# Where weighing stands among the score products, and one slot's delay of the low parts, in a five-layer attention kernel

## The chip, the cores and the metric

The program runs on 1 core of one Trainium2 chip. The time is the device time of one execution in microseconds. PE is TensorE, DVE is VectorE, ACT is ScalarE, POOL is GpSimd, SP is SyncE, which issues the DMA transfers.

## What is computed

x has 32 sequences of 128 tokens with 128 features. Five attention layers with 16 heads of 8 features follow each other, with a perceptron after the second and the last, and a routed mixture of three experts between the second and the third:

```python
def _attn(q, k, v, mask):
    s = jnp.einsum('bqhd,bkhd->bhqk', q, k) * scale
    s = jnp.where(mask, s, jnp.finfo(s.dtype).min)
    a = jax.nn.softmax(s, axis=-1)
    return jnp.einsum('bhqk,bkhd->bqhd', a, v)
```

l0: self attention with rotary positions and a query-key mask (128 keys). l0c: cross attention to 77 context tokens, with a key mask. l2: cross attention, 77 keys, no mask. l3s: self attention, 128 keys, no mask. l3c: cross attention, 77 keys, no mask. The layers with 128 keys are called wide here, those with 77 narrow. Each layer is x + attention(norm(x)) times its output weights, in f32.

## The kernel before, in words

One sequence of one layer is a job; four jobs are a quad. There are 8 quads a layer and 40 in all, 160 jobs. Every engine runs the same loop over slots t. In slot t the exact scores of job t are made; qi is t // 4 and cl is t % 4. All engines have their instructions in an order written out by hand, and semaphores join them. Phase 0 is l0 and l0c, phase 1 the other three; the routed mixture lies between.

A job goes through these steps:

- POOL `spread_k(t+7)` (L1952) puts the keys of one job into a block form, `kblk_r`, which has two buffers.
- PE `rows(t+5, 1)` and `rows(t+6, 0)` (L658, in l0c also L653, in l0 with `mask_rows`, L634) make the row scores of heads 8 to 15 of one job and heads 0 to 7 of the next. Both use the same two banks of PSUM, `row_scores`.
- DVE `row_max` (L1242) takes the negated maximum of each row. The next use of the banks waits for it.
- Once a quad, ACT rounds the maxima (L1738), POOL splits off their low part, PE turns them (`turn_max`, L666) and DVE spreads them (`spread_max`, L1249).
- PE `exact(t)` (L695, 16 products of 32 rows) and `shift(t, h)` (L710) make the scores with the row maximum subtracted, in l0 with `mask_scores` (L676). `exact(t)` waits until ACT has taken both halves of job t-1.
- ACT `exponentiate(t, h)` (L1758) takes half 0 and half 1, 1024 columns each.
- PE `weigh(t-1)` (L725, 32 products) multiplies with the values; DVE `turn_blocks` (L1258), `invert` (L1263) and `turn_back` (L1270), and POOL `normalise(t-2)` (L1995) follow.
- `quad_work` on PE has what comes once a quad: projections of k for quad qi+2 at cl 0 (L605), of v (L613) and of the output (L620) at cl 2, of q for quad qi+3 at cl 3 (L594), the transposes of norms at cl 1, some at cl 3 (L572). In the wide layers the function `quad_ahead` does a part of it, half projections among them, between the subtractions and the row scores.

The exact scores are made from high and low parts of q and k. ACT `round_q` (L1673, cl 1) and `round_k(qi+2)` (L1683, cl 3, between the two exponentials of that slot) make the high parts; POOL `split_q` (L1935) and `split_k` (L1943) subtract them to get the low ones. There is one buffer each for `k_high`, `q_low` and `k_low`. SP `stack_pair(m)` (L2157, L2160) then copies high and low parts of two jobs into a ring of three pairs with 8 transfers; it waits for both splits of the quad. `round_k` and `split_q` of the next quad wait for the landing of both pairs of this quad:

```python
def round_k(q):
    w.wait_ge(k_split, q)
    if q:
        w.wait_ge(*pair_landed(2 * q - 2))
        w.wait_ge(*pair_landed(2 * q - 1))
```

In POOL's slot the order is: rotated halves of l0 (`add_rotated`, L1959, L1962, at cl 0 and 1), `spread_k(t+7)`, `split_max` (cl 2), `normalise(t-2)`, the two splits, `shift_normed` (L1983), `normalise_x` (L1969, L1972; for the norm that PE turns at cl 1 it stands in cl 0), sums into x.

Of the kernel before, what the change touches and what calls it, by code (L numbers as in the profile page):

```python
# [17 lines left out]
B, S, D = 32, 128, 128  # L18
# [72 lines left out]
def layer_of(q):  # L91
    return LAYERS[q // NB]
# [92 lines left out]
def build(nc, a, out_x):  # L185
    with ExitStack() as ctx:
# [343 lines left out]
        def tensor_program(e):  # L530
# [26 lines left out]
            def keep_busy(times, bank):  # L557

                for _ in range(times):
                    e.matmul(bank, ident, W["ones"], start=True, stop=True)  # L560
# [191 lines left out]
            def attention(phase, first=-16, last=None):  # L752
# [32 lines left out]
                        else:  # L785
                            w.wait_ge(q_done, qi + 3 - NB + 1)

                def is_wide(t):

                    return t in jobs and layer_of(t // QUAD).nk == S  # L790

                def quad_ahead(qi, cl):

                    for back in range(1, QUAD + 1):
                        quads_read(QUAD * qi + cl - back)
                    if cl == 0 and qi + 2 in quads:
                        project_k(qi + 2, slice(0, 2))
                    if cl == 2 and qi - 2 in quads:
                        project_out(qi - 2)
                    if cl == 3 and qi + 3 in quads:  # L800
                        project_q(qi + 3, slice(0, QUAD if layer_of(qi).rope else 2))

                def quad_work(t, qi, cl):
                    early = max(min(2 * t + 1, 8 * hi), 8 * lo)
                    if cl == 2 and qi + 1 in quads:
                        w.wait_ge(exp_done, early)
                        project_v(qi + 1)
                    if t in norm_at and not turned_in_quads(norm_at[t]):
                        w.wait_ge(exp_done, early)
                        turn_normed(norm_at[t])  # L810
                    if t == -2 * QUAD:
                        project_k(0)
                    if cl in (0, 3) or t in norm_at or cl == 1 and qi + 3 in quads or cl == 2 and qi - 2 in quads:
                        for back in range(1, QUAD + 1):
                            quads_read(t - back)
                    rest = slice(2 if is_wide(t) else 0, QUAD)
                    if cl == 0 and qi + 2 in quads and t != -2 * QUAD:
                        project_k(qi + 2, rest)
                    if cl == 1 and qi + 3 in quads and layer_of(qi + 3).name == "l3c":
                        turn_x(qi + 3)  # L820
                    if t in norm_at and turned_in_quads(norm_at[t]):
                        turn_normed(norm_at[t])
                    if cl == 2 and qi - 2 in quads and not is_wide(t):
                        if qi >= hi:
                            w.wait_ge(exp_done, early)
                        project_out(qi - 2)
                    if cl == 3 and qi + 3 in quads and not (is_wide(t) and layer_of(qi).rope):
                        project_q(qi + 3, rest)

                for t in range(4 * lo + first, end):  # L830
                    qi, cl = divmod(t, QUAD)
                    masked = t in jobs and layer_of(qi).mask == "qk"
                    if t + 5 in jobs:
                        mask_rows(t + 5, 1, True)
                    if t in (4 * lo, 4 * lo + 1):
                        w.wait_ge(max_done, 8 * lo + 8)
                    if masked:
                        scores_read(t - 1)
                        mask_scores(t, 0)
                    if t + 5 in jobs:  # L840
                        rows(t + 5, 1)
                    scores_read(t - 1)
                    if t in jobs:
                        exact(t)
                        shift(t, 0)
                        shift(t, 1)
                    if is_wide(t):
                        quad_ahead(qi, cl)
                    if phase == 1 and t in (4 * lo - 2, 4 * lo - 1):
                        keep_busy(4, av_bank[:, 0:128])  # L850
                    if t + 6 in jobs:
                        rows(t + 6, 0)
                    if masked:
                        mask_rows(t + 6, 0, False)
                        mask_scores(t, 1)
                        if cl == 3 and qi + 1 in quads:
                            w.wait_ge(nblk_done, qi + 2)
                    if masked or is_wide(t) and cl == 2:
                        quad_work(t, qi, cl)
                        if t - 1 in jobs:  # L860
                            weigh(t - 1)
                    else:
                        if t == 4 * hi:
                            first_layer(phase, 0, hi, range(2))
                        if t - 1 in jobs:
                            weigh(t - 1)
                        if t + 6 in jobs:
                            mask_rows(t + 6, 0, False)
                        if t in (-6, -4, -3):
                            keep_busy(3, scores[:, 0, 0:128])  # L870
                        if cl == 3 and qi + 1 in quads:
                            turn_max(qi + 1)
                        quad_work(t, qi, cl)
                    if masked and cl == 2 and qi + 1 in quads:
                        turn_max(qi + 1)
                    if phase == 0 and last is None:
                        first_prototypes(t - 4 * hi)
                    if t == -11:
                        modulate(range(2, 9))
                    if t == -8:  # L880
                        gates_and_context()
                    if t == -7:
                        w.wait_ge(act_setup, ACT_AT["l0mod1"])
                        keep_busy(5, scores[:, 0, 0:128])
                    c = first_layer_at(t, hi)
                    if c is not None:
                        first_layer(phase, c, hi, range(0 if c else 2, 4))
                    if second_layer_at(t, hi) is not None:
                        second_layer(phase, second_layer_at(t, hi), hi)
                    if phase == 0 and folding_at(t, hi) is not None:  # L890
                        fold_weights(folding_at(t, hi))
# [1020 lines left out]
        def pool_program(e):  # L1912
# [102 lines left out]
            def attention(phase, first=-16, last=None):  # L2015
# [4 lines left out]
                for t in range(4 * lo + first, end):  # L2020
# [8 lines left out]
                        split_max(qi + 1)  # L2029
                    if t - 2 in jobs:  # L2030
                        normalise(t - 2)
                    if cl == 3 and qi + 2 in quads:
                        split_q(qi + 2)
                        split_k(qi + 2)
                    if t - 1 in norm_at and not affine_by_act(norm_at[t - 1]):
                        shift_normed(norm_at[t - 1])
                    for it in XHAT_AT.get((phase == 1, t), ()):
# [278 lines left out]
```

## Time and profile before

| | us |
|---|---|
| median of 3 runs | 1069.88 |
| lowest and highest | 1067.48, 4715.3 |
| the profiled execution | 1063.98 |
| its span | 1061.8 |
| mean granted TensorE clock | 0.952 |

The profiled execution's own time is 2.2 us more than the span from its first to its last instruction. The clock has two levels, 2.4 GHz (1.00) and 1.2 GHz (0.50). In a timeline row the number after the start is the duration; in brackets stand the idle time of the engine before the row and what ended it.

### The profile page before, as it was taken

What the parts mean: (1) busy time and instruction counts of PE and PEld (TensorE: products, weight loads), DVE (VectorE), ACT (ScalarE), POOL (GpSimd) and SP (SyncE); (2) the same over time, 40 slices, a digit from 0 to 9 for tenths busy, and PEclk for the clock granted to TensorE, in tenths of its full rate; (3) what the DMA queues carried; (4) which work ended last, traced back from release to release, by engine and by line L of the source; (5) the groups of instructions that cost most, each with busy time, mean ns of one, the idle gap of its engine ahead of it and who ended that gap; (6) DMA issues with size and microseconds to landing.
All of it is one profiled execution on the core that took longest, in us unless ns stands there. A gap on an engine that the chain in (4) does not pass through costs nothing.

```text
span 1061.8 us, 32084 instructions
## 1 busy us (share of the span) xinstructions
PE 971.6 (91%) x13009; PEld 670.9 (63%) x13009; DVE 749.7 (71%) x1852; ACT 623.6 (59%) x938; POOL 616.5 (58%) x739
## 2 busy tenths in 40 slices
PE   7898898998889999999999988888999998888998
PEld 5455565666566776676776655655666666566676
DVE  7767888777875444677787768877898766776421
ACT  2144455577767555545554567775677677775752
POOL 6657888576874332111113779776778655685520
PEclk9569999999997999999999989998999999997999
DMA  6613333434332102000000133333334333333011
GB/s 215 219 65 112 120 108 107 133 107 134 125 120 74 41 30 98 9 10 7 7 7 19 59 116 107 123 107 103 131 112 145 116 125 119 110 98 121 7 40 40
DMA packets 101459, 96.89 MB, mean 91 GB/s; under 512 B 11632, under 2 KB 93808, under 8 KB 100928
## 3 DMA queue, kind: packets, MB, share of 16 engines
q1 hardware_dynamic: 101312, 94.84, 26.9%
q8 instruction: 103, 1.69, 0.7%
q14 instruction: 44, 0.36, 0.1%
HBM read 18.77 MB, written 2.15 MB: 20 GB/s over the span
## 4 chain that ended last, share of the span: by engine, by line
PE 68%; DVE 14%; issue 8%; POOL 7%; ACT 1%; SPq 1%; DMA 0%; POOLq 0%; DVEq 0%; ACTq 0%
PE weighed L725 13%; DVE negmax L1242 8%; PE row_scores L658 8%; PE scores L921 6%; PE weighed L748 5%; PE scores L613 4%; PE row_scores L921 3%; PE quads L620 3%; POOL kblk_r L1952 3%; PE quads L594 2%; PE row_scores L738 2%; PE scores L738 2%; PE quads L605 2%; PE row_scores L634 2%; PE weighed L938 2%
## 5 line engine op out<-in xcount | busy, mean ns | idle before, releaser
L1242 DVE TENSOR_REDUCE negmax<-row_scores 128x8 f32<-128x616 f32 (+1 forms) x312 | 298.5, 957 | 101.4 <-PE row_scores L658 74.4
L1758 ACT ACTIVATE p<-scores 128x1024 f32<-128x1024 f32 (+1 forms) x253 | 253.1, 1019 | 123.4 <-PE scores L710 87.7
L1952 POOL TENSOR_TENSOR kblk_r<-work,pack_const 128x308 fp32r<-128x308 f32 (+1 forms) x160 | 133.6, 836 | 113.0 <-PE row_scores L658 92.1
L658 PE MATMUL row_scores<-kblk_r,qr 32*128 32x308 f32 (+1 forms) x624 | 145.5, 457 | 52.4 <-DVE negmax L1242 42.4
L725 PE MATMUL weighed<-p,v 77*32 77x128 f32 (+1 forms) x5120 | 184.4, 288 | 1.8 <-DVE nat L1258 1.3
L725 PEld LDWEIGHTS weighed<-p,v 77*32 77x32 f32 (+1 forms) x5120 | 137.9, 114 | 36.1 <-issue 27.2
L658 PEld LDWEIGHTS row_scores<-kblk_r,qr 32*128 32x128 f32 x624 | 63.9, 191 | 130.2 <-issue 84.6
L695 PE MATMUL scores<-q_ring,k_ring 32*77 32x128 f32 (+1 forms) x2512 | 123.0, 256 | 4.4 <-ACT shared L1695 1.7
L695 PEld LDWEIGHTS scores<-q_ring,k_ring 32*77 32x77 f32 (+1 forms) x2512 | 100.0, 167 | 7.9 <-ACT shared L1695 1.9
L1258 DVE STREAM_TRANSPOSE nat<-weighed 128x256 f32<-128x256 f32 x160 | 70.9, 443 | 41.8 <-PE weighed L725 37.1
L710 PE MATMUL scores<-nblk,select 32*77 32x512 bf16 (+1 forms) x628 | 93.1, 396 | 0.0
L1995 POOL TENSOR_TENSOR attn<-nat,rden 128x128 f32<-128x128 f32 x160 | 64.7, 404 | 43.4 <-DVE rden L1263 41.2
L1758 ACT ACTIVATE p<-scores,neg_kb 77x1024 f32<-77x1024 f32 x61 | 65.8, 1105 | 15.8 <-PE scores L710 12.9
L1969 POOL TENSOR_TENSOR xh<-x,mv 128x512 f32<-128x512 f32 x48 | 50.0, 1041 | 25.6 <-ACT rst L1657 25.6
L748 PEld LDWEIGHTS weighed<-layers_w,work 128*128 128x128 f32 x512 | 59.0, 192 | 3.6 <-issue 2.4
L1972 POOL TENSOR_TENSOR xh<-xh,rst 128x512 f32<-128x512 f32 (+1 forms) x56 | 58.2, 1040 | 4.4
L748 PE MATMUL weighed<-layers_w,work 128*128 128x128 f32 x512 | 59.9, 275 | 0.8 <-DVE x L1299 0.8
L2068 POOL TENSOR_TENSOR xh<-x,r_mv 128x512 f32<-128x512 f32 x8 | 8.3, 1042 | 80.5 <-ACT r_rst L1665 79.6
L1935 POOL TENSOR_TENSOR work<-work,qr 128x512 f32<-128x512 f32 x40 | 50.8, 1270 | 4.9 <-DMA q_ring<-qr 4.9
L594 PE MATMUL quads<-work,layers_w 128*128 128x512 f32 (+1 forms) x96 | 48.3, 586 | 0.0
L1746 ACT COPY v<-scores 77x512 f32<-77x512 f32 (+1 forms) x40 | 23.3, 583 | 37.1 <-PE scores L613 37.0
L1131 DVE BATCH_NORM_STATS2 bn<-x 128x6 f32<-128x128 f32 x192 | 43.9, 268 | 0.6 <-POOL x L2007 0.6
(334 smaller groups left out, 1958.1 us busy)
## 6 DMA issues: line engine op xcount, KB each, us to landing
q_ring<-work SPq DMA_DIRECT2D x160, 128.0 KB, 2.1
q_ring<-qr SPq DMA_DIRECT2D x160, 128.0 KB, 2.1
k_ring<-k_high SPq DMA_DIRECT2D x64, 128.0 KB, 2.1
k_ring<-work SPq DMA_DIRECT2D x64, 128.0 KB, 2.1
k_ring<-k_high SPq DMA_DIRECT2D x96, 77.0 KB, 2.0
k_ring<-work SPq DMA_DIRECT2D x96, 77.0 KB, 2.0
shared<-gates_hbm SPq DMA_DIRECT2D x24, 256.0 KB, 3.1
shared<-in_ctx_tok SPq DMA_DIRECT2D x15, 154.0 KB
```

The lines of the kernel that those rows point to most:

```text
L594: mm = e.matmul(quad_bank[:, at], W[layer.wq], xn[q % 3][:, at], start=True, stop=True)
L658: mm = e.matmul(row_banks(n, h)[:, i, 0:cols], qr[q % 3][at, s * S:(s + 1) * S], kblk_r[n % 2][at, 0:cols], start=layer.mask is None or ma ...
L695: mm = e.matmul(score_banks(n, g // 2)[0:nk, g % 2, j * S:(j + 1) * S], keys_of(m, nk)[at, j, half * nk:(half + 1) * nk].bitcast(F32R), q_ ...
L710: mm = e.matmul(score_banks(n, h)[0:nk, i, :], select[at, s, 0:nk], nblk[q % 2][at, :], start=False, stop=not masked_after, skip_group_che ...
L725: mm = e.matmul(av_bank[TILE * j:TILE * j + TILE, i2 * S:(i2 + 1) * S], v[0:nk, at:at + TILE], p[n % 2][0:nk, g * NJ + j, :], start=i1 == ...
L748: mm = e.matmul(mlp_out_bank[:, s * D:(s + 1) * D], mlp_h[c % 2][k][:, s * S:(s + 1) * S], W[weight][:, k * D:(k + 1) * D], start=(k == 0) ...
L921: mm = e.matmul(bank, weight, src, start=(part == 0), stop=(part == 1))
L1242: e.tensor_reduce(negmax[q % 2][:, 2 * h:2 * h + 2, s * NJ:(s + 1) * NJ], row_banks(n, h)[:, :, 0:NJ * nk].rearrange("p g (j k) -> p g j k ...
L1258: e.transpose(nat[n % 2][:, :, :].rearrange("p c (i s) -> p (c i) s", i=NG), av_bank[:, weighed_cols].rearrange("p (i b s) -> p b i s", i= ...
L1758: e.activation(p[n % 2][0:nk, 8 * h:8 * h + 8, :], score_banks(n, h)[0:nk].rearrange("p g (j q) -> p (g j) q", j=NJ), ACT.Exp, bias=hide, ...
L1952: e.tensor_tensor(kblk_r[n % 2][:, 0:NJ * nk].rearrange("p (j k) -> p j k", j=NJ), k_of[q % 2][:, s * nk:(s + 1) * nk].unsqueeze(1).to_bro ...
L1995: e.tensor_tensor(attn[n % 2][:, :].rearrange("p (k d) -> p k d", d=HD), nat[n % 2][:, :, :].rearrange("p i (k c) -> p (i k) c", c=16)[:, ...
```

## The change

On PE, `weigh(t-1)` moves to directly behind the subtractions in every slot, ahead of `rows(t+6, 0)`. In l0, `mask_scores(t, 1)` comes directly behind the subtractions too. `quad_ahead` goes; its parts go back whole into `quad_work` at the end of the slot. On POOL, `split_q` and `split_k` of a quad run in cl 0 of the next slot, behind `spread_k` and `normalise` of that slot, where they ran in cl 3. The first quad of each phase keeps its place.

```diff
-                def is_wide(t):
-                    return t in jobs and layer_of(t // QUAD).nk == S
-                def quad_ahead(qi, cl):
-                    for back in range(1, QUAD + 1):
-                        quads_read(QUAD * qi + cl - back)
-                    if cl == 0 and qi + 2 in quads:
-                        project_k(qi + 2, slice(0, 2))
-                    if cl == 2 and qi - 2 in quads:
-                        project_out(qi - 2)
-                    if cl == 3 and qi + 3 in quads:
-                        project_q(qi + 3, slice(0, QUAD if layer_of(qi).rope else 2))
...
-                    rest = slice(2 if is_wide(t) else 0, QUAD)
                     if cl == 0 and qi + 2 in quads and t != -2 * QUAD:
-                        project_k(qi + 2, rest)
+                        project_k(qi + 2)
...
-                    if cl == 2 and qi - 2 in quads and not is_wide(t):
+                    if cl == 2 and qi - 2 in quads:
                         if qi >= hi:
                             w.wait_ge(exp_done, early)
                         project_out(qi - 2)
-                    if cl == 3 and qi + 3 in quads and not (is_wide(t) and layer_of(qi).rope):
-                        project_q(qi + 3, rest)
+                    if cl == 3 and qi + 3 in quads:
+                        project_q(qi + 3)
...
                         exact(t)
                         shift(t, 0)
                         shift(t, 1)
-                    if is_wide(t):
-                        quad_ahead(qi, cl)
-                    if phase == 1 and t in (4 * lo - 2, 4 * lo - 1):
-                        keep_busy(4, av_bank[:, 0:128])
-                    if t + 6 in jobs:
-                        rows(t + 6, 0)
                     if masked:
-                        mask_rows(t + 6, 0, False)
                         mask_scores(t, 1)
                         if cl == 3 and qi + 1 in quads:
                             w.wait_ge(nblk_done, qi + 2)
-                    if masked or is_wide(t) and cl == 2:
-                        quad_work(t, qi, cl)
-                        if t - 1 in jobs:
-                            weigh(t - 1)
-                    else:
-                        if t == 4 * hi:
-                            first_layer(phase, 0, hi, range(2))
-                        if t - 1 in jobs:
-                            weigh(t - 1)
-                        if t + 6 in jobs:
-                            mask_rows(t + 6, 0, False)
-                        if t in (-6, -4, -3):
-                            keep_busy(3, scores[:, 0, 0:128])
-                        if cl == 3 and qi + 1 in quads:
-                            turn_max(qi + 1)
-                        quad_work(t, qi, cl)
+                    if phase == 1 and t in (4 * lo - 2, 4 * lo - 1):
+                        keep_busy(4, av_bank[:, 0:128])
+                    if t == 4 * hi:
+                        first_layer(phase, 0, hi, range(2))
+                    if t - 1 in jobs:
+                        weigh(t - 1)
+                    if t + 6 in jobs:
+                        rows(t + 6, 0)
+                        mask_rows(t + 6, 0, False)
+                    if t in (-6, -4, -3):
+                        keep_busy(3, scores[:, 0, 0:128])
+                    if not masked and cl == 3 and qi + 1 in quads:
+                        turn_max(qi + 1)
+                    quad_work(t, qi, cl)
                     if masked and cl == 2 and qi + 1 in quads:
                         turn_max(qi + 1)
...
                     if t - 2 in jobs:
                         normalise(t - 2)
-                    if cl == 3 and qi + 2 in quads:
-                        split_q(qi + 2)
-                        split_k(qi + 2)
+                    if t == 4 * lo - 5:
+                        split_q(lo)
+                        split_k(lo)
+                    if cl == 0 and qi + 1 in quads and qi + 1 != lo:
+                        split_q(qi + 1)
+                        split_k(qi + 1)
```

## Rows read from the trace of the kernel before

**Rows 1.** The page, part 1: PE's busy time, share and instructions.
```profile
PE 971.6 (91%) x13009; PEld 670.9 (63%) x13009; DVE 749.7 (71%) x1852; ACT 623.6 (59%) x938; POOL 616.5 (58%) x739
```

**Rows 2.** Windows over 3, 6, 6, 8 and 5 whole quads; busy time by engine.
```profile
121.70:183.30 61.60, 55.42 (x1153) 35.58 (x1137) 52.65 (x112) 31.98 (x43) 52.73 (x58) 1.00 0.35 118
219.80:314.50 94.70, 81.61 (x1602) 57.40 (x1598) 75.92 (x197) 69.21 (x98) 70.00 (x96) 1.00 0.40 125
630.60:723.70 93.10, 80.19 (x1503) 55.29 (x1502) 78.36 (x213) 67.37 (x102) 76.51 (x102) 1.00 0.35 112
744.20:875.90 131.70, 122.48 (x2031) 87.26 (x2030) 109.53 (x209) 93.45 (x130) 95.80 (x117) 1.00 0.38 127
875.90:952.70 76.80, 66.97 (x1255) 46.88 (x1257) 55.24 (x127) 57.26 (x82) 50.34 (x70) 1.00 0.35 112
```

**Rows 3.** Timeline of PE, one narrow slot of l2, cl 1.
```profile
664.74 0.41 PE L658 MATMUL row_scores<-kblk_r,qr 32*128 32x308 f32 x2
...
666.14 0.40 PE L658 MATMUL row_scores<-kblk_r,qr 32*128 32x308 f32 x2 [0.51 <-DVE negmax L1242]
666.47 1.08 PE L725 MATMUL weighed<-p,v 77*32 77x128 f32 x32
667.48 0.66 PE L572 MATMUL quads<-pack_const,xh 128*128 128x128 f32 x4
668.07 0.41 PE L658 MATMUL row_scores<-kblk_r,qr 32*128 32x308 f32 x2
```

**Rows 4.** Timeline of DVE, the same slot.
```profile
665.19 0.80 DVE L1242 TENSOR_REDUCE negmax<-row_scores 128x8 f32<-128x616 f32 x1 [0.19 <-PE row_scores L658]
```

**Rows 5.** Timelines of POOL, DVE and SP in l3s, a wide quad.
```profile
777.91 1.28 POOL L1943 TENSOR_TENSOR work<-work,k_high 128x512 f32<-128x512 f32 x1
...
780.75 1.23 DVE L1242 TENSOR_REDUCE negmax<-row_scores 128x8 f32<-128x1024 f32 x1 [0.35 <-PE row_scores L658]
...
789.26 1.25 SPq L2160 DMA_DIRECT2D q_ring<-qr  x2
```

**Rows 6.** Timeline of POOL: two successive quads' splits, l3c.
```profile
875.73 0.84 POOL L1943 TENSOR_TENSOR work<-work,k_high 128x308 f32<-128x308 f32 x1
...
889.31 1.27 POOL L1935 TENSOR_TENSOR work<-work,qr 128x512 f32<-128x512 f32 x1 [0.56 <-DMA q_ring<-qr]
```

**Rows 7.** Timeline of SP: first and last of a quad's 16 transfers.
```profile
876.63 0.53 SPq L2157 DMA_DIRECT2D k_ring<-k_high  x1
...
886.44 1.25 SPq L2160 DMA_DIRECT2D q_ring<-qr  x2
```

**Rows 8.** Timeline of ACT at cl 3 of that quad.
```profile
889.25 0.45 ACT L1683 CAST k_high<-work 128x308 fp32r<-128x308 f32 x1 [0.61 <-DMA q_ring<-qr]
889.60 1.01 ACT L1758 ACTIVATE p<-scores 77x1024 f32<-77x1024 f32 x1
```

**Rows 9.** Timeline of PE: the next quad's first exact scores.
```profile
890.69 0.53 PE L695 MATMUL scores<-q_ring,k_ring 32*77 32x128 f32 x12
```

**Rows 10.** Waits over the whole span: us in total, times, longest.
```profile
ACT k_high L1683 <- DMA q_ring<-qr: 6.5, 10, 2.3
```

**Rows 11.** Timeline of POOL: cl 0 in l0, and in l2 from 661.2.
```profile
143.85 1.28 POOL L1959 TENSOR_TENSOR rot<-rot,sin_live 128x512 f32<-128x512 f32 x1
...
661.59 0.70 POOL L1952 TENSOR_TENSOR kblk_r<-work,pack_const 128x308 fp32r<-128x308 f32 x1
662.77 0.40 POOL L1995 TENSOR_TENSOR attn<-nat,rden 128x128 f32<-128x128 f32 x1 [0.48 <-DVE rden L1263]
```

**Rows 12.** Windows over two quads of l0; the granted clock stands third from the end.
```profile
77.80:99.80 22.00, 18.86 (x391) 12.03 (x375) 17.13 (x37) 10.44 (x14) 16.34 (x19) 0.92 0.29 98
121.70:142.30 20.60, 18.54 (x399) 11.91 (x383) 17.63 (x38) 10.50 (x14) 17.64 (x20) 1.00 0.34 117
```

**Rows 13.** Timeline of PE in l0, and the window at the lower level behind it.
```profile
90.20 0.50 PE L658 MATMUL row_scores<-kblk_r,qr 32*128 32x512 f32 x2 [1.11 <-DVE negmax L1242]
...
90.60:94.00 3.40, 3.40 (x42) 2.67 (x44) 1.86 (x5) 1.70 (x3) 1.47 (x3) 0.50 0.24 82
```

## The prediction

> **What bounds the kernel now.** The page's busy line comes first: PE is busy 91% of the span, DVE 71%, ACT 59%, POOL 58% [rows 1]. No engine is full, so the question is which wait ends last in a slot (one job's turn through all engines). The windows over whole runs of quads of one layer (a quad is four slots, cl 0 to 3) give the unit that I count in [rows 2]: layer l0 61.6/3 = 20.5 us a quad, l0c 94.7/6 = 15.8, l2 93.1/6 = 15.5, l3s 131.7/8 = 16.5, l3c 76.8/5 = 15.4. Together they are the larger part of the span, and the change touches nothing else by more than a slot.
>
> Then the timeline of one narrow slot (l2, cl 1) [rows 3]. The row scores of half 1 start at 664.74, exact scores and subtractions follow at once; then PE idles 0.51 us until 666.14, when row scores of half 0 may overwrite the two banks that DVE has just read: DVE's maximum runs 665.19 to 665.99 [rows 4]. Weighing starts 0.33 us later, the transposes 1.01 us after that, and the next slot at 668.07: 3.33 us in all. From row scores to row scores is thus at least 1.40 us in a narrow slot, and in a wide one about 1.90, as the maximum takes 1.23 [rows 5].
>
> Last the chain behind the two DMA groups of a quad. POOL's split of k ends at 876.57 [rows 6]. SP then issues 16 transfers, 876.63 to 887.69, without a break [rows 7]. At 889.25 ACT's rounding of the next k starts after a 0.61 us wait that the last of them ended, and POOL's next split of q at 889.31 likewise [rows 6, 8]. The exponential of half 1 stands behind that rounding on ACT (889.60 to 890.61), and PE's next exact scores start at 890.69 [rows 9]. So this quad was already held by its transfers: split end to landing 12.6 us, landing to next exact scores 1.5 us. The table of waits has ten such waits, 6.5 us in all [rows 10]: there is next to no slack now.
>
> **Weighing before the row scores of half 0.** No instruction is added to the narrow slots; two pieces change places. After the subtractions PE can go on at once: its next piece may start about 0.83 us after the slot's start (666.14 less 0.51, less the overlap seen between any two pieces). Weighing then holds 1.01 us, row scores 0 start at 1.84, other quad work at 2.18. The maximum of half 0 now has only that quad work to hide behind: the next slot can't start before 1.84 + 1.40 = 3.24. Hence cl 0 and cl 1 cost 3.24 (3.33 to 3.5 now); cl 2, with two projections of eight matmuls, loses its idle 0.5 and costs 4.1; cl 3 costs 3.3 to 3.6. PE alone would need 13.9 us a narrow quad, where it takes 15.4 to 15.8. In the wide l3s the same sum is 2.05 + 1.90 = 3.96 for three slots and 4.66 for cl 2: 16.5, as now, for there half a projection already stands in the first gap, and it is taken out. In l0 the maximum of half 0 has little cover left in cl 0, 1 and 3: 5.0 each and 5.7, so 20.7 against 20.5.
>
> **Mask products behind the subtractions, projections whole.** The eight mask products are the same eight; behind the subtractions they let the exponential of half 1 start about 1.5 us earlier. ACT is busy 32 of 61.6 us there [rows 2], and l0's slots end on the maximum, so I take nothing. Halved projections become whole. What that saves in set-up no row shows; I bound it by 0.5 us a quad either way, the idle of one slot [rows 3], and take 0, since in those slots PE waits for the maximum anyway.
>
> **Low parts split one slot later.** This is the term that decides. The splits of q and k move from POOL's cl 3 to cl 0 of the next slot, behind that slot's spreading of k and its normalising. Both wait for the new slot: in l2 spreading started 0.4 us after the slot's start at 661.2, and normalising ended at 663.17, 2.0 us in, held by the reciprocal of DVE [rows 11]. The splits then take 1.27 and 0.83 us [rows 6], so they end 4.05 us after the slot's first row scores, where the one at 876.57 ended 0.7 us after its slot's start at 875.9 [rows 2, 6]. In a wide layer it is 2.4 + 1.27 + 1.28 = 4.9 [rows 5], in l0 about 7.5, because two rotations of 1.28 us and a spreading stand ahead of it there [rows 11]. Behind the splits are queued on POOL the shift and the centring of the next norm, for which PE's transposes of cl 1 wait; they come 2 us later too. And SP's two groups of eight wait for them: 12.6 us again from split to landing in a narrow quad, 12.8 in l3s (split end 779.19, last issue ends 790.51, plus the same 1.5) [rows 5], some 13.5 in l0.
>
> Counted from row scores of cl 0 (call it P): landing at 4.05 + 12.65 = 16.7, next quad's exact scores at 16.7 + 1.55 = 18.25. PE would have been there at 13.9. ACT's exponential of cl 3 is stuck behind the rounding for the difference.
>
> Not all of it is lost. P is the row scores of cl 0, and PE issues them ahead of the exact scores that wait; nothing on DVE and POOL up to the splits needs the stuck exponential. So a quad that starts its exact scores late by s has its splits early by s. Two successive quads take 18.25 + 13.9 = 32.1 together, 16.1 each. By layer, with the quads that have both a split and a later rounding in them:
> l0c 16.1 against 15.8, 6 quads, +2; l2 16.1 against 15.5, 7 quads, +4; l3c 16.1 against 15.4, 6 quads, +4; l3s (4.9 + 12.8 + 1.75 + 16.5)/2 = 18.0 against 16.5, 7 quads, +10.5; l0 (7.5 + 13.5 + 1.75 + 20.7)/2 = 21.7 against 20.5, 7 quads, +8.5. Sum +29 us.
>
> The late centring costs nothing on top while s is over about 1.6 us; below it, up to 0.5 us in cl 1, which I leave inside the range.
>
> **The clock.** An idle of PE of 1.11 us before 90.20 was followed by the lower level, 1.2 GHz, for 3.4 us, and that quad took 22.0 us where its neighbour at 2.4 GHz took 20.6 [rows 12, 13]. The new idle at each quad's start is s, 1 to 3 us, so I expect such a fall in two of three of the 33 quads. Each costs 1.5 us of PE's time, of which half passes through the mean of the two periods above: 22 x 0.75 = +16; some land where PE waits anyway, so I take +13.
>
> **A rule of the notes.** The Trainium skill, DMA: Bandwidth & Descriptors, section Rules for kernel authors, says to issue a transfer early, compute, and wait on its semaphore late. By that rule this move is wrong, and the trace agrees in so far as the wait at 889.25 is a wait for a landing. The page gives no figure that the sum uses.
>
> **The sum.** The profiled run took 1063.98 us with a span of 1061.8. 1064 + 29 + 13 = 1106. The median of the three runs shown is 1069.88, 5.9 above the profiled one; I carry that along: 1112 us.
>
> **Rivals.**
> 1. *PE doesn't run ahead.* If row scores of cl 0, or DVE and POOL behind them, are held by the stuck exponential after all, every quad takes the whole chain: narrow 18.25 - 15.6 = 2.65 x 19 = +50, l3s 3.0 x 7 = +21, l0 2.3 x 7 = +16: 1157 us. For it: POOL is in order and busy 86% of l0 [rows 2]. Against: in program order no such wait stands before P. Chance 0.15.
> 2. *The chain is nearly covered.* If POOL reaches its splits 1 us earlier than I count, and the clock holds, the excess halves: +12 to +18, 1082 to 1088. For it: SP's issue, not POOL, is most of the 12.6 us, and may run quicker when the groups meet less traffic. Chance 0.22.
> 3. *Faster.* The landing falls before ACT asks for it, because the chain starts from a slot that itself begins sooner. Then narrow quads are held by PE, or by DVE's scaling at the end of cl 3, and take 14.5: -1.1 x 19 = -21, l0 +1, 1050 us. It decides where splits end by 0.6 us after the slot's start instead of 4. Against: the two POOL steps ahead wait for that very slot's row scores and reciprocal. Chance 0.13.
> 4. My forecast, 1095 to 1130: 0.50.
>
> A measurement of this kernel can tell about 2%, 21 us. Faster by over 2% is rival 3, 0.13; within 2% is rival 2 and a sliver, 0.22; slower 0.65. The range leaves out rival 3 and the upper half of rival 1: 1062 to 1150.
>
> **What would show it.** In the changed profile: the rounding of k idle before it on DMA in nearly every quad, 1 to 4 us each (now ten times, 6.5 us in all), 50 us or more in sum; PE's exact scores of cl 0 idle on ACT's exponential; the idle of PE's row scores on the maximum down in cl 2 and 3 and moved to half 1 in cl 0 and 1; narrow quads near 16.1, l3s near 18.0, and the mean granted clock below 0.95. The prediction is wrong if rounding waits stay at a few us: then my POOL order is at fault. If the waits are there but quads alternate by less, it is the running ahead that I have mis-sized.

## The result, and the profile after

The changed kernel takes 1179.38 us (median of four runs, 1169.86 to 1201.65) against 1069.38 us for the kernel before on the same chip: ratio 1.1005, 95% interval 1.0913 to 1.1098. Here and below a time is the median of all runs, while a ratio leaves out single runs of a kernel that took over 1.5% longer than its fastest, such as the 4715.3 us above, so the two need not divide exactly. The forecast was 1112 us with a range of 1062 to 1150: right in its sign, far too small in its size. Fences of the kernel after are from a profiled execution of 1176.95 us.

Parts 1, 2 and 4 of the page after: busy time, the granted clock in 40 slices, the chain by engine.
```profile
PE 1074.7 (91%) x12961; PEld 725.9 (62%) x12961; DVE 744.3 (63%) x1852; ACT 622.1 (53%) x938; POOL 618.1 (53%) x739
...
PEclk9669968988777999999999667887889987876899
...
PE 60%; POOL 12%; SPq 9%; issue 8%; DVE 6%; DMA 2%; ACT 2%; POOLq 0%; ACTq 0%; DVEq 0%
```
The same line of the page before:
```profile
PEclk9569999999997999999999989998999999997999
```
DVE, ACT and POOL are busy as long as before, to 6 us. PE is busy for 1074.7 us where it was 971.6 [rows 1], with 48 fewer records of matmuls. PE's work has not grown, it runs slower: sixes, sevens and eights stand where nines stood, in most of the slices that hold attention quads, and not in the middle of the span. From the mean granted clock (0.856 after, 0.952 before) the time at the lower level, 1.2 GHz, is 2 x (1 - clock) x span: 338 us after, 102 before.

The waits of the kernel after (us in total, times, longest):
```profile
PE scores L695 <- ACT p L1733: 31.2, 12, 4.6
PE quads L572 <- POOL xh L1947: 17.7, 16, 1.8
PE row_scores L658 <- DVE negmax L1217: 13.4, 34, 1.4
...
ACT k_high L1658 <- DMA q_ring<-qr: 53.1, 20, 5.0
```
and two of the kernel before:
```profile
PE row_scores L658 <- DVE negmax L1242: 42.4, 75, 1.4
...
PE quads L572 <- POOL xh L1972: 1.0, 1, 1.0
```
The order on PE does what it was changed for: the wait for the maximum fell from 42.4 to 13.4 us. What is left of it stands before half 1, 0.18 and 0.32 us in the quad at 963.5, as forecast. In its place stand a wait of ACT's rounding for the transfers (6.5 us in ten [rows 10], now 53.1 in twenty), behind it PE's exact scores waiting for ACT's exponential, and the transposes of the norm waiting for POOL's centring.

The chain of one quad of l3c (timelines of four engines; the start, the duration, and in brackets the idle before):
```profile
963.52 0.41 PE L658 MATMUL row_scores<-kblk_r,qr 32*128 32x308 f32 x2
...
965.59 1.27 POOL L1910 TENSOR_TENSOR work<-work,qr 128x512 f32<-128x512 f32 x1
...
966.82 0.84 POOL L1918 TENSOR_TENSOR work<-work,k_high 128x308 f32<-128x308 f32 x1
...
967.72 0.53 SPq L2135 DMA_DIRECT2D k_ring<-k_high  x1
...
977.15 0.41 PE L658 MATMUL row_scores<-kblk_r,qr 32*128 32x308 f32 x2
...
977.52 1.25 SPq L2138 DMA_DIRECT2D q_ring<-qr  x2
...
980.33 0.45 ACT L1658 CAST k_high<-work 128x308 fp32r<-128x308 f32 x1 [4.64 <-DMA q_ring<-qr]
980.68 1.01 ACT L1733 ACTIVATE p<-scores 77x1024 f32<-77x1024 f32 x1
...
981.75 0.57 PE L695 MATMUL scores<-q_ring,k_ring 32*77 32x128 f32 x16 [4.19 <-ACT p L1733]
```
Row scores at 963.52, splits done at 967.66, landing at 980.33, exact scores at 981.75: 4.14 + 12.67 + 1.42 = 18.23 us, where the forecast worked out 4.05 + 12.65 + 1.55 = 18.25. The row scores of the next cl 0 started at 977.15, 4.6 us ahead of the stalled exact scores, so PE does run ahead.

Windows of the kernel after: four successive l3c quads; then the 17.1 us behind that 4.19 us idle; then the five layers' stretches (l0 8 quads, l0c 7, l2 8, l3s 8, l3c 6). The granted clock stands third from the end.
```profile
963.50:981.70 18.20, 13.56 (x252) 9.33 (x251) 11.45 (x26) 11.82 (x17) 11.51 (x17) 1.00 0.30 95
981.70:1002.20 20.50, 20.45 (x247) 14.04 (x247) 7.80 (x17) 11.58 (x16) 6.79 (x10) 0.58 0.26 84
1002.20:1020.80 18.60, 13.57 (x252) 9.33 (x251) 12.40 (x29) 11.24 (x16) 10.31 (x16) 0.97 0.29 93
1020.80:1043.30 22.50, 22.22 (x253) 15.32 (x253) 10.54 (x26) 11.81 (x18) 9.02 (x13) 0.57 0.24 76
...
982.00:999.10 17.10, 17.10 (x194) 12.03 (x189) 5.73 (x12) 8.53 (x13) 4.15 (x7) 0.50 0.32 100
...
50.10:239.00 188.90, 175.09 (x2906) 104.60 (x2890) 132.30 (x281) 82.30 (x117) 126.16 (x142) 0.84 0.29 97
239.00:372.80 133.80, 119.94 (x1842) 84.50 (x1842) 82.68 (x219) 78.52 (x110) 78.74 (x106) 0.76 0.32 103
654.90:812.30 157.40, 145.82 (x1960) 97.92 (x1960) 103.55 (x274) 90.02 (x137) 100.50 (x131) 0.71 0.29 92
812.30:963.50 151.20, 132.16 (x1992) 89.00 (x1992) 107.54 (x208) 93.37 (x129) 97.17 (x117) 0.89 0.33 110
963.50:1082.20 118.70, 102.97 (x1503) 71.21 (x1502) 66.41 (x159) 68.31 (x97) 62.37 (x86) 0.77 0.27 87
```
The first four rows hold the mistake. In l3c, and in l3s too, quads of two kinds alternate. One runs at 2.4 GHz: PE is busy 13.6 us (the forecast's 13.9) and then waits for the chain to close at 18.2 to 18.6. The other runs behind that wait: PE works without a gap, 20.45 of 20.50 us, but at 0.58 of full speed, and passes the moment of its own landing long after it. The pair takes 38.7 and 41.1 us, not 32.1. By layer, against the same stretches before (168.6, 111.8, 130.7, 131.7 and 93.9 us): +20.3, +22.0, +26.7, +19.5 and +24.8, in all +113 us, which is the whole loss.

The other layers don't alternate so plainly. In l0 ACT's rounding waits in three successive quads (1.79, 2.71 and 3.25 us), and 20.4 us at 1.2 GHz follow the third. l2, with the largest loss, runs its first two quads at 1.2 GHz, behind an idle of 1.94 us that stands in the kernel before as well, with 1.70 us. There 10.1 us at the lower level followed it, here 44.3:
```profile
654.40:698.70 44.30, 43.58 (x470) 27.67 (x472) 24.69 (x73) 23.36 (x39) 26.86 (x34) 0.50 0.27 85
```

### The profile page after: what moved, and what is told of

It reads as the page before. It is cut to its first block, busy times and chain, and to the rows that moved or that the text cites. A ratio compares the mean times of both kernels' runs of the same rounds, so it can differ in the third digit from the quotient of the medians.

```text
span 1174.8 us, 32004 instructions
## 1 busy us (share of the span) xinstructions
PE 1074.7 (91%) x12961; PEld 725.9 (62%) x12961; DVE 744.3 (63%) x1852; ACT 622.1 (53%) x938; POOL 618.1 (53%) x739
## 3 DMA queue, kind: packets, MB, share of 16 engines
HBM read 18.77 MB, written 2.15 MB: 18 GB/s over the span
## 4 chain that ended last, share of the span: by engine, by line
PE 60%; POOL 12%; SPq 9%; issue 8%; DVE 6%; DMA 2%; ACT 2%; POOLq 0%; ACTq 0%; DVEq 0%
PE weighed L725 11%; PE scores L896 6%; PE row_scores L658 5%; PE weighed L748 5%; SPq L2135 4%; SPq L2138 4%; PE scores L695 4%; PE scores L613 3%; PE scores L710 3%; DVE negmax L1217 3%; PE row_scores L896 3%; PE quads L620 2%; POOL kblk_r L1927 2%; DMA q_ring<-qr 2%; PE quads L605 2%
## 5 line engine op out<-in xcount | busy, mean ns | idle before, releaser
L725 PE MATMUL weighed<-p,v 77*32 77x128 f32 (+1 forms) x5120 | 213.9, 319 | 2.1 <-DVE nat L1233 1.3
L725 PEld LDWEIGHTS weighed<-p,v 77*32 77x32 f32 (+1 forms) x5120 | 157.4, 127 | 57.9 <-issue 45.1
L658 PE MATMUL row_scores<-kblk_r,qr 32*128 32x308 f32 (+1 forms) x624 | 161.0, 511 | 16.6 <-DVE negmax L1217 13.4
L695 PE MATMUL scores<-q_ring,k_ring 32*77 32x128 f32 (+1 forms) x2512 | 136.4, 284 | 39.4 <-ACT p L1733 31.2
L695 PEld LDWEIGHTS scores<-q_ring,k_ring 32*77 32x77 f32 (+1 forms) x2512 | 112.1, 194 | 48.0 <-ACT p L1733 35.9
L658 PEld LDWEIGHTS row_scores<-kblk_r,qr 32*128 32x128 f32 x624 | 68.5, 214 | 104.1 <-DVE negmax L1217 49.9
L710 PE MATMUL scores<-nblk,select 32*77 32x512 bf16 (+1 forms) x628 | 104.2, 463 | 0.0
L620 PE MATMUL quads<-layers_w,attnT 128*128 128x128 f32 x288 | 49.1, 327 | 0.0
L1658 ACT CAST k_high<-work 128x308 fp32r<-128x308 f32 (+1 forms) x40 | 20.5, 511 | 53.2 <-DMA q_ring<-qr 53.1
```

The lines of the kernel that those rows point to most:

```text
L620: mm = e.matmul(out_bank(q)[:, s * D:(s + 1) * D], attnT[q % 2][:, s * S:(s + 1) * S], W[layer_of(q).wo], start=True, stop=True)
L658: mm = e.matmul(row_banks(n, h)[:, i, 0:cols], qr[q % 3][at, s * S:(s + 1) * S], kblk_r[n % 2][at, 0:cols], start=layer.mask is None or ma ...
L695: mm = e.matmul(score_banks(n, g // 2)[0:nk, g % 2, j * S:(j + 1) * S], keys_of(m, nk)[at, j, half * nk:(half + 1) * nk].bitcast(F32R), q_ ...
L710: mm = e.matmul(score_banks(n, h)[0:nk, i, :], select[at, s, 0:nk], nblk[q % 2][at, :], start=False, stop=not masked_after, skip_group_che ...
L725: mm = e.matmul(av_bank[TILE * j:TILE * j + TILE, i2 * S:(i2 + 1) * S], v[0:nk, at:at + TILE], p[n % 2][0:nk, g * NJ + j, :], start=i1 == ...
```

## Experiments

All medians are set against runs of the kernel before on the same chip; the ratio has its 95% interval in brackets. Four things vary: where the splits stand, the order on PE, extra products, and who waits for which transfers. Two theories stood at the start. A: the splits' later slot lengthens the chain to the transfers, PE waits at each quad's start, and the clock that falls behind the wait makes the larger part of the loss. B: the new order on PE makes the loss by itself.

**The two halves of the change.** e1 takes the change and puts the splits back into cl 3; e2 takes the kernel before and moves the splits alone.
```diff
 e1, from the kernel after (e2: the reverse edit, from the kernel before)
-                    if t == 4 * lo - 5:
-                        split_q(lo)
-                        split_k(lo)
-                    if cl == 0 and qi + 1 in quads and qi + 1 != lo:
-                        split_q(qi + 1)
-                        split_k(qi + 1)
+                    if cl == 3 and qi + 2 in quads:
+                        split_q(qi + 2)
+                        split_k(qi + 2)
```


> Only the order on PE is changed; the splits stand in cl 3 as before. Theory A (the later splits delay the landing that ACT's rounding waits for, and the idle that follows drops PE's clock): rounding waits stay at a few us, narrow quads at 14.9 to 15.3, l3s at 16.5, 1050 to 1075 us, clock about 0.95. Theory B (the order on PE costs, by the maximum of half 0 that has lost its cover): over 1130 us, still slow.

> Only the splits move to cl 0 of the next slot; PE keeps the order of before. Theory A: rounding waits of 40 us or more, idle ahead of exact scores, clock below 0.88, 1140 to 1190 us. Theory B: within 2% of before, 1050 to 1090 us.

e1: 1096.84 us, 1.0275 [1.025, 1.03]. e2: 1187.98 us, 1.1109 [1.1033, 1.1184]. One edit on POOL, in the old order of PE, costs all that the whole change costs, so B is not the cause of the 110 us. But e1 is not at 1050 to 1075 as A wanted either: with the splits where they were, the new order still loses 2.75%, 30 us against the 1066.55 of before on that chip. Windows of e1: its eight l3s quads, its eight l2 quads.
```profile
771.90:902.10 130.20, 118.97 (x1998) 81.66 (x1998) 108.83 (x212) 93.65 (x130) 95.99 (x118) 1.00 0.38 128
...
618.90:771.90 153.00, 146.54 (x1960) 97.56 (x1961) 103.57 (x274) 89.96 (x137) 101.67 (x132) 0.70 0.30 95
```
The wide layer is at full clock and level with before (131.7). The narrow l2 takes 153.0 us against 130.7, at a clock of 0.70. PE and ACT of e1 in narrow layers, and e1's total of the wait for a landing:
```profile
715.06 0.50 PE L695 MATMUL scores<-q_ring,k_ring 32*77 32x128 f32 x16 [2.15 <-ACT p L1733]
...
915.74 0.45 ACT L1658 CAST k_high<-work 128x308 fp32r<-128x308 f32 x1 [1.70 <-DMA q_ring<-qr]
...
ACT k_high L1658 <- DMA q_ring<-qr: 25.0, 13, 3.8
```
A faster PE now reaches the next rounding before the unchanged transfers have landed. The chain of [rows 6 to 9] had next to no slack, and what the new order saves on PE turns into idle at the quad's start, with a clock that falls behind it. The longest stretch, 61 of e1's 215 us at 1.2 GHz, stands at l2's first exact scores. They idle 2.20 us there, where the kernel before idles 1.70 us and has 10.1 us at the lower level. Why this stretch lasts so long stays open.
```profile
618.30:679.70 61.40, 60.55 (x646) 39.73 (x646) 34.41 (x103) 32.20 (x53) 39.84 (x51) 0.50 0.28 89
```

**Is it the length of the wait or the clock?** e3 fills the wait. It gives PE eight dead products of 128 columns (16 records in the trace) ahead of the exact scores of each quad's cl 0, but for the first quad of a phase; their results are overwritten. They add work and shorten no chain; the clock is the one thing that they were meant to help. e15 is the control: the same products in the kernel before.
```diff
 e3, from the kernel after; e15, from the kernel before (in masked slots ahead of mask_scores(t, 0))
                         rows(t + 5, 1)
                     scores_read(t - 1)
+                    if t in jobs and cl == 0 and qi != lo and not masked:
+                        w.wait_ge(exp_done, 2 * t - 1)
+                        keep_busy(8, scores[:, 0, 0:128])
```


> The changed kernel with eight more 128-column products on PE at each quad's start, ahead of the exact scores that wait; their results are overwritten. They are about 1.8 us of added work a quad. If the fall of the clock is most of the loss beyond the landing chain: less time at 1.2 GHz, above all in l3c and l3s, and 1120 to 1150 us, faster than the changed kernel in spite of the added work. If the clock is only a by-product: 33 quads x 0 to 1.8 us more, 1180 to 1240 us.

> The control for the added products: the kernel before with the same eight products at each quad's start. It has hardly any idle there, so they are plain work: in l3s 2.1 us a quad, in narrow quads 0.5 to 2 us, since 0.5 us of ACT's wait and some idle take them in: 1090 to 1125 us. If the added products themselves speed a quad up in some way other than the clock, it stays under 1075 us.

e3: 1123.4 us, 1.0534 [1.05, 1.0568], 56 us faster than the changed kernel that does less. e15: 1117.44 us, 1.048 [1.0407, 1.0553]. With the products in both, the change costs 6 us instead of 110. e3's page, its waits, ACT and PE at one quad's start, and windows over eight l3s and four l3c quads:
```profile
PEclk9659999999998999999999979999999999997999
...
ACT k_high L1664 <- DMA q_ring<-qr: 75.3, 34, 4.3
...
958.41 0.45 ACT L1664 CAST k_high<-work 128x308 fp32r<-128x308 f32 x1 [2.19 <-DMA q_ring<-qr]
...
958.02 2.05 PE L560 MATMUL scores<-pack_const 128*128 128x128 f32 x16
960.00 0.50 PE L695 MATMUL scores<-q_ring,k_ring 32*77 32x128 f32 x16
...
781.70:928.00 146.30, 135.31 (x2124) 95.94 (x2124) 106.82 (x207) 93.78 (x129) 97.31 (x119) 1.00 0.34 114
928.00:993.20 65.20, 61.80 (x1069) 44.34 (x1068) 41.86 (x97) 45.43 (x64) 37.99 (x54) 1.00 0.33 106
```
The wait for the landing is longer in sum than in the changed kernel, 75.3 against 53.1 us and 34 times against 20: with no quad slowed, PE and ACT are early at nearly every landing. The stretches shown hold their clock at 1.00; in the whole run 106 us are left at 1.2 GHz, where the changed kernel had 338 and the kernel before 102. The quads are now 65.2/4 = 16.3 us and 146.3/8 = 18.3 us, where the forecast's chain had given 16.1 and 18.0. That fits the sum over the chain, at a clock that holds.

The control must be read with care: the products are not free in a kernel that has nothing to fill. e15's l3c quads take 16.7 us against 15.4:
```profile
923.60:990.50 66.90, 61.07 (x1065) 44.43 (x1064) 43.70 (x97) 45.31 (x64) 37.73 (x55) 1.00 0.32 101
```
Five of its l3s quads at full clock take 91.8/5 = 18.4. So the 6 us are not the price of the late splits by themselves: e3 is 5.3% slower than the kernel before without products. Nor do e3's 16.3 and 18.3 us prove the chain's sum, since the products alone take the quads of e15 as far.

e8 puts six such products into e1.

> The changed order on PE, splits back in cl 3, six added products at each quad's start. Theory A: the added products fill the idle in which the clock falls, under 130 us at 1.2 GHz (216 without them), 1060 to 1085 us in spite of about 1.3 us of added work a quad. Theory C: 1100 us or more.

It takes 1095.82 us, 1.029 [1.0223, 1.0357], as e1 does, although its time at 1.2 GHz fell from 215 to 92 us (mean clock 0.902 and 0.958, spans 1098.6 and 1094.0). The products themselves took back what the clock gave. e8's eight l2 quads take 135.0 us where e1's take 153.0, but its eight l3s quads, at full clock in both, take 141.6 where e1's take 130.2:
```profile
631.10:766.10 135.00, 128.86 (x2060) 89.11 (x2060) 104.47 (x277) 90.20 (x137) 103.55 (x134) 0.92 0.34 107
766.10:907.70 141.60, 131.67 (x2093) 92.38 (x2092) 107.17 (x210) 93.77 (x129) 96.34 (x118) 1.00 0.35 118
```
Inconclusive on the size of the clock's part, a plain miss on the time.

**Take the wait away instead.** e4 gives the rounded k two buffers in the changed kernel, so that ACT's rounding waits for transfers of the quad before the last; e5 does so in e1.
```diff
-        k_high = sb("k_high", [128, QUAD * S], F32R)
+        k_high = [sb(f"k_high{i}", [128, QUAD * S], F32R) for i in range(2)]
...
-                w.wait_ge(k_split, q)
-                if q:
-                    w.wait_ge(*pair_landed(2 * q - 2))
-                    w.wait_ge(*pair_landed(2 * q - 1))
+                w.wait_ge(k_split, q - 1)
+                if q > 1:
+                    w.wait_ge(*pair_landed(2 * q - 4))
+                    w.wait_ge(*pair_landed(2 * q - 3))
...  the copy, k's split and SP's transfers take k_high[q % 2]
```


> The changed kernel with two buffers for the high part of k, so that ACT's rounding waits for the landing of the quad before the last. The splits keep their place and their waits. Theory A: ACT's rounding no longer waits, exact scores don't idle at the quad's start, narrow quads 14.9 to 15.5, l3s about 17, the clock back over 0.93, 1050 to 1085 us. Theory B: no gain, over 1150 us.

> The changed order on PE, splits back in cl 3, and two buffers for the high part of k. With the splits back alone it took 1097 us, all of the loss in the narrow layers (l0 and l3s are shorter than before). Theory A (in narrow quads a faster PE runs into the landing, waits 1 to 2 us behind ACT's rounding, and the clock falls): without ACT's wait those idles go, clock over 0.94, 1040 to 1065 us. Theory C (the narrow order itself costs, or the clock falls from smaller idles too): 1085 us or more.

e4: 1100.91 us, 1.0284 [1.0218, 1.0351]: it wins 78 us of the 110, short of what was expected. e5: 1063.64 us, 0.9948 [0.9911, 0.9986], inside what theory A expected: without ACT's wait the 2.75% of e1 are gone. What is left in e4 is in its waits, and in windows over a stretch of l0c and one of l3s:
```profile
PE quads L572 <- POOL xh L1947: 28.6, 24, 2.4
...
230.00:350.00 120.00, 108.33 (x1764) 77.72 (x1752) 81.81 (x218) 76.10 (x107) 77.00 (x105) 0.80 0.35 112
...
760.00:890.00 130.00, 118.58 (x1998) 81.83 (x1996) 111.39 (x216) 93.28 (x130) 97.37 (x118) 1.00 0.39 131
```
ACT's landing wait is gone, l3s holds its clock, and l0c and l2 don't: there the transposes of cl 1 wait 0.7 to 2.4 us at a time for the centring queued on POOL behind the late splits. In l3s the same wait is 0.8 us a quad, with no fall behind it. This is the "late centring" that the forecast had booked at nothing. It sits in the changed kernel too, 17.7 us in 16 waits; one of them on PE, and the stretch behind it:
```profile
703.38 0.41 PE L658 MATMUL row_scores<-kblk_r,qr 32*128 32x308 f32 x2
705.23 0.79 PE L572 MATMUL quads<-pack_const,xh 128*128 128x128 f32 x4 [1.44 <-POOL xh L1947]
...
705.30:709.00 3.70, 3.70 (x58) 2.70 (x58) 1.79 (x5) 2.30 (x5) 3.26 (x6) 0.53 0.51 165
```

**The wide layers by themselves.** e7 keeps the splits in cl 3 and takes the new order of PE in wide slots only.
```diff
 e7, from e1
+                    wide = t in jobs and layer_of(qi).nk == S
-                    if t - 1 in jobs:
+                    if t - 1 in jobs and wide:
                         weigh(t - 1)
                     if t + 6 in jobs:
                         rows(t + 6, 0)
-                        mask_rows(t + 6, 0, False)
+                        if wide:
+                            mask_rows(t + 6, 0, False)
+                    if t - 1 in jobs and not wide:
+                        weigh(t - 1)
+                    if t + 6 in jobs and not wide:
+                        mask_rows(t + 6, 0, False)
```


> Splits in cl 3; the changed order on PE in the wide layers alone, the narrow slots keep the order of before. Theory A: wide layers as in the run with the splits back (l0 156 instead of 165 us, l3s 125 instead of 127.5), narrow layers as before, 1050 to 1062 us. Theory C says the same of the narrow layers; if the wide gain came from something else, 1065 to 1075.

1071.9 us, 1.0034 [0.9998, 1.0069]: nothing, where 1050 to 1062 was expected. In wide slots the new order is worth nothing, as the prediction had it and as this expectation had not. The expectation had taken a shorter l0 of e1 for the order's work. But three of e1's l0 quads at full clock take 62.1 us, 20.7 each, against 20.5 before [rows 2]; the difference lay in the clock at the start of l0, where the kernel before runs at 1.2 GHz from 25.8 to 73.4 us while e1's l0 has a mean of 1.00:
```profile
112.30:174.40 62.10, 57.68 (x1151) 35.19 (x1135) 52.99 (x112) 30.95 (x43) 52.67 (x58) 1.00 0.35 117
```

**Shorten the chain at its other end.** The rounding of k has to wait only for the transfers that read the rounded k, which SP issues first in each pair. In e11 (from e1) the key transfers count on semaphores of their own, the rounding and k's split wait for those alone, and k is split before q; the exact scores wait for both semaphores. e12 is the same edit in the kernel before, e13 in the changed kernel with its splits in cl 0, e14 is e11 with the two buffers of e5.
```diff
 e11, from e1
+        def keys_landed(m):
+            return ld[f"keys{m % PAIRS}"], 16 * len(PARTS) * (m // PAIRS + 1)
...  round_k and split_k
-                    w.wait_ge(*pair_landed(2 * q - 2))
-                    w.wait_ge(*pair_landed(2 * q - 1))
+                    w.wait_ge(*keys_landed(2 * q - 2))
+                    w.wait_ge(*keys_landed(2 * q - 1))
...  SP
-                    e.dma_start(keys_of(m, nk)[x:128:NJ, :, :], k_src[:, k_at]).then_inc(landed, 16)
+                    e.dma_start(keys_of(m, nk)[x:128:NJ, :, :], k_src[:, k_at]).then_inc(keys_landed(m)[0], 16)
```


> The changed order on PE, splits back in cl 3 with k's first, and the four transfers of keys of a pair on a semaphore of their own, so that ACT's rounding waits for those alone; the four of q are issued 2.6 us later. Theory A: the chain is 2 to 3 us shorter, rounding waits near zero, narrow quads 14.0 to 14.9, clock over 0.94, 1030 to 1060 us. If the landing chain isn't what narrow quads run into, 1085 us or more.

> The kernel before, with k's splits first and the key transfers on a semaphore of their own (the edit that took the changed order with splits in cl 3 to 0.981 of before). Theory A, with PE of before needing 15.3 to 15.7 us a narrow quad by itself: the landing wait goes (6.5 us in all), 1055 to 1066 us. If the gain of the earlier run came from the shorter chain and not from the order on PE: 1045 to 1052 us.

> The changed kernel, splits in cl 0, with k's first and the key transfers on their own semaphore. The chain ends 2.6 us earlier and k's split 1.27 us earlier. Theory A: of the 2.2 us of mean wait a narrow quad nearly all goes, idles at the quad's start under 1 us; what stays are the late centring at cl 1 and its falls of the clock, 1075 to 1110 us. If the chain isn't the cause: over 1150 us.

> Changed order on PE, splits in cl 3, key transfers on their own semaphore, and two buffers for the high part of k. If any landing wait of ACT still costs, 5 to 15 us less than with one buffer (1049 us); if the narrow quads are now held by PE and by DVE at the end of cl 3, the same within 5 us.

e11: 1048.8 us, 0.9808 [0.9755, 0.9861]. e12: 1062.92 us, 0.9933 [0.9897, 0.997]. e13: 1108.06 us, 1.0293 [1.0217, 1.0369]. e14: 1055.84 us, 0.9809 [0.9749, 0.987], a ratio no other than e11's. e11 beats both kernels, by 1.9% with an interval from 1.4 to 2.5%, and the intervals of e11 and e12 lie apart, so about 1.2% of it is the new order of PE, which in e1 cost 2.75%. In e13 the splits in cl 0 still cost 5% over e11; its trace, of a run of 1124.91 us, has 18.4 us of transposes waiting for the centring, in 17 waits, and 20.0 us of rounding waiting for key transfers. Four l3c quads of e11:
```profile
867.30:923.00 55.70, 53.46 (x1003) 37.17 (x1002) 41.97 (x97) 46.46 (x65) 38.57 (x54) 1.00 0.39 123
```
55.7/4 = 13.9 us a quad, just what the forecast had worked out for PE alone, at full clock.

## Why the prediction was wrong

**The step that failed is "The clock", the +13 us.** The forecast took from one event before (1.11 us idle, 3.4 us at the lower level [rows 12, 13]) that each fall costs 1.5 us of PE's time, of which half passes through. Its number of falls, 22, was high rather than low: 21 stretches at 1.2 GHz begin inside the five layers, where the kernel before has 6. Their length was wrong. They last 3.4 to 44.4 us, 307 us in all against 63 before. At 981.75 stood 4.19 us of idle, then 17.1 us at 1.2 GHz with PE busy for all of it, 8.5 us of PE's work lost at one quad's start. The kernel before could have warned: the event taken was of the shortest kind in its own trace, where idles of 0.56 and 0.42 us (before 314.50 and 315.63) and of 1.70 us (before 613.49) stand ahead of much longer stretches:
```profile
315.90:329.40 13.50, 13.31 (x172) 10.14 (x172) 6.38 (x19) 6.80 (x10) 5.08 (x8) 0.50 0.40 127
616.30:626.40 10.10, 10.03 (x122) 7.25 (x122) 6.60 (x24) 5.28 (x9) 6.29 (x9) 0.50 0.47 152
```
The term was also halved, on the ground that a chain-bound quad forgives a slow PE. It does only up to the slack, and a quad at half clock is not bound by its chain any more: 20.5 us where the chain alone wants 18.25 less the 4.2 of head start. Against the forecast's total without the clock (1064 + 29 + 5.9 = 1099), the rest is 80 us where 13 stood. That splits a total by a forecast, not by a measurement; what is measured is that filling the wait with work gave back 56 us, net of the work, as the time at the lower level fell by 232 us, back to what the kernel before has.

**Running ahead** was right as a mechanism and half right in its effect. In l3c the exact scores of one quad wait 4.2 us and those of the next not at all, as in the forecast's own sum of a whole chain and a quad of PE's 13.9 us; its clock term then counted with s, 1 to 3 us, at every quad's start. What came was a head start that the slowed PE then used up.

**The chain** was right to 0.15 us in each of its three parts in l3c (the 1.55 us from landing to exact scores is 1.44 by [rows 8, 9], and 1.42 after), and with it the places of the waits: the landing wait at 53.1 us (50 or more forecast), though in 20 quads and not in nearly every one, the exact scores idle on the exponential, the wait for the maximum down. The granted clock fell below 0.95, as said; how far was not. Narrow quads at 16.1 and l3s at 18.0 came only in e3, at 16.3 and 18.3, where the added products alone explain as much.

**"The late centring costs nothing"** was wrong. It was argued from s over 1.6 us; in l3s and l3c every second quad has s near 0, and in l2 most quads. It is 17.7 us of idle, the longest of them in l2, with the lower level behind the one shown, and it is the largest PE wait left in e4 once the landing wait is gone.

**PE's 13.9 us a narrow quad** was right, and hidden: e11 shows it, and e1 shows why it can't be collected even with the splits in place. **Wide slots as now** was right (e7, e1). That the mask products and whole projections are worth nothing was not tried by itself; l0's quads in e1, 20.7 us as forecast, fit it. The wide and l0 chains rest on three terms for which the forecast showed no full rows, 7.5, 13.5 and 1.75 us; no experiment prices them one by one.

**The rivals.** PE not running ahead (1157) gave the time nearest to the result, by a mechanism that the timeline refutes: the row scores at 977.15 stand ahead of the stalled exact scores. Its time was near by luck. A nearly covered chain and a faster kernel are refuted by the chain of 18.23 us and by the ratio.

## What to carry to other kernels

When a producer of transfers moves by a slot, follow its chain to the next loop's first consumer, through every in-order engine on the way: here a rounding that waited for transfers it did not depend on held the exponential behind it, and the cure was to count transfers by what they read, not to speed up an engine. Where PE is the bound, price an idle of a few us not at its own length but at the lower clock that can follow it, from all the falls in the trace and not from one, and look at what the next stage does at half speed. A faster order on the bounding engine gains only as far as the waits beside it have slack; measure that slack first.

## What the runs showed of the hardware

Once fallen, the clock stayed low although PE was busy all the time: 17.1 us at 0.50 with PE busy 17.10 of 17.10 us, after an idle of 4.19 us; before the change 3.4 us had followed 1.11 us. Nor is every idle followed by a fall: in e3 the exact scores at 698.24 had waited 1.32 us, and the clock stayed at 1.00 from 690 to 711 us. In e1 2.15 us of idle were followed by 15.8 us at a mean of 0.57, PE busy throughout:
```profile
715.20:731.00 15.80, 15.80 (x196) 11.37 (x198) 7.20 (x19) 8.33 (x13) 8.33 (x12) 0.57 0.34 108
```
The Trainium skill, TensorE: Matmul & The Clock Gate, Part 1, says that the clock depends on how busy PE has been of late; the trace agrees in that a fall follows an idle, and shows that a busy PE alone doesn't bring the clock back at once. How the length of the low stretch follows from the idle before it stays open: these are single stretches, not a series. 2 us of useless products a quad made a kernel of 1179 us 56 us faster.
